# Attention results leave through device memory by head dimension and are normalised there, in an AdaLN block with attention and a mixture of experts

## What is computed

```python
h = layernorm(x) * (1 + ca) + sa
x = x + ga * attention(h)            # 2 x 2048 tokens, 16 heads of 16, causal
h = layernorm(x) * (1 + cb) + sb
x = x + gb * mixture(h)              # 8 experts, 512 tokens each

scores = relu(q @ k.T) * R_hat       # R_hat depends on the distance and the head
attn = softmax(where(causal, -inf, scores) / 4)
ctx = attn @ v ; ctx = ctx @ Wo + bo
```

## Time and profile before

| | us |
|---|---|
| median of 3 runs | 1761.94 (1759.61 to 1763.59) |
| the profiled execution's own time | 1759.48 |
| its span, first to last instruction | 1757.7 |
| busy in it: TensorE, VectorE, ScalarE, POOL | 1481.0, 1182.5, 1022.6, 931.5 |

### The profile page before, as it was taken

How to read it: one execution, slowest core, us unless ns; L and a number is a source line. 1 busy time by engine, 2 the same in 40 slices (tenths; PEclk the granted TensorE clock), 3 DMA queues, 4 the chain that set the end, 5 groups by cost and what they waited for, 6 DMA issues and landing times. The chain is left out here.

```text
span 1757.7 us, 43162 instructions
## 1 busy us (share of the span) xinstructions
PE 1481.0 (84%) x16098; PEld 1137.3 (65%) x16318; DVE 1182.5 (67%) x3764; ACT 1022.6 (58%) x1796; POOL 931.5 (53%) x1460
## 2 busy tenths in 40 slices
PE   5977999999999999999999998999985514999897
PEld 3544777777777777777777777777764304566565
DVE  7626778777877788778877787778749883122121
ACT  3435777777777777777777777777745500211211
POOL 3324766676567756676667666765656401223322
PEclk9987999999999999999999999999997655999999
DMA  6342121112211221121112211121022231334431
GB/s 206 112 143 97 60 80 58 50 54 82 61 50 52 78 64 53 50 78 64 55 50 67 72 58 50 55 81 62 2 97 81 96 120 26 75 78 106 113 81 21
DMA packets 68587, 129.06 MB, mean 73 GB/s; under 512 B 9392, under 2 KB 52288, under 8 KB 64288
## 3 DMA queue, kind: packets, MB, share of 16 engines
q1 hardware_dynamic: 60688, 115.38, 21.0%
q0 software_dynamic: 6464, 9.29, 3.0%
q10 hardware_dynamic: 1232, 1.71, 0.3%
HBM read 100.91 MB, written 25.44 MB: 72 GB/s over the span
## 5 line engine op out<-in xcount | busy, mean ns | idle before, releaser
L719 ACT ACTIVATE region_p<-turn_ps 128x512 f32<-128x512 f32 x512 | 303.6, 602 | 175.7 <-PE turn_ps L678 170.5
L719 ACT ACTIVATE region_o<-turn_ps 128x512 f32<-128x512 f32 x576 | 339.7, 601 | 110.5 <-PE turn_ps L678 105.1
L667 PE MATMUL score_ps<-region_s 128*128 128x384 bf16 (+3 forms) x1060 | 347.0, 347 | 33.1 <-DVE maxima L752 29.4
L678 PE MATMUL turn_ps<-ident,region_a 128*128 128x128 f32 x2048 | 342.4, 274 | 27.7 <-DVE region_c L772 22.7
L678 PE MATMUL turn_ps<-ident,region_x 128*128 128x128 f32 x2048 | 343.3, 275 | 26.3 <-DVE region_c L772 17.9
L794 POOL TENSOR_SCALAR region_a<-region_a,maxima 128x1152 f32<-128x1152 f32 (+6 forms) x224 | 271.9, 1214 | 125.7 <-ACT region_a L726 112.7
L752 DVE CUSTOM_DVE_ANT_0 region_x<-score_ps,region_t,maxima 128x512 f32<-128x512 f32 (+1 forms) x416 | 281.4, 707 | 74.5 <-PE score_ps L667 73.0
L678 PEld LDWEIGHTS turn_ps<-ident,region_a 128*128 128x128 f32 x2048 | 259.3, 141 | 58.8 <-DVE region_c L772 28.0
L678 PEld LDWEIGHTS turn_ps<-ident,region_x 128*128 128x128 f32 x2048 | 254.0, 141 | 60.4 <-DVE region_c L772 29.9
L752 DVE CUSTOM_DVE_ANT_0 region_a<-score_ps,region_t,maxima 128x512 f32<-128x512 f32 (+1 forms) x352 | 241.3, 699 | 47.0 <-remote 27.7
L752 DVE CUSTOM_DVE_ANT_0 region_a<-score_ps,region_t 128x384 f32<-128x384 f32 (+2 forms) x256 | 139.1, 553 | 87.9 <-PE score_ps L667 87.9
(11 more groups left out here) (198 smaller groups left out, 2104.1 us busy)
## 6 DMA issues: line engine op xcount, KB each, us to landing
region_t<-factor_rows SPq DMA_DIRECT2D x32, 1024.0 KB
region_x<-in_fc_t SPq DMA_DIRECT2D x16, 1024.0 KB, 8.1
region_s<-q_split SPq DMA_DIRECT2D x64, 192.0 KB
region_s<-k_split SPq DMA_DIRECT2D x64, 192.0 KB
region_x<-in_x SPq DMA_DIRECT2D x8, 1024.0 KB, 11.7
q_split<-region_o SPq DMA_DIRECT2D x16, 384.0 KB, 2.7
k_split<-region_t SPq DMA_DIRECT2D x16, 384.0 KB, 2.6
region_s<-q_split SPq DMA_DIRECT2D x32, 128.0 KB
```

Of the source, the lines that this page charges most:

```text
L667: nc.tensor.matmul(score_ps[:, j % SB, 0:(hi - lo) * P], stacks[:, b, 0, t * P:(t + 1) * P], stacks[:, b, 1, lo * P:hi * P], start=True, s ...
L678: last = nc.tensor.transpose(turn_ps[:, ring_at[what, j] % TB, q * P:(q + 1) * P], rows[t][:, k * P:(k + 1) * P], ident[:, :])
L719: nc.scalar.activation(weight(j), turn_ps[:, ring_at[what, j] % TB, :], ACT.Exp).then_inc(exp_done, 1)
```

## The change

The results of a group are no longer turned back. After `save`, SP stores the 17 rows of each stream to a tensor `heads_out` (head, 16 dimensions and sum, token) in device memory, 4 DMAs a group. They are read back as `context`, now laid out by model dimension (128 partitions) and token, with every sum repeated for its 16 partitions by a broadcasting read, and VectorE divides there: one reciprocal and one multiply of 128x1024 for each of eight groups of 512 tokens. The projection takes this layout as it is.

Events and places:

- `back`, `recip`, `norm` and `wait_ring` go. A turn waits only for the exponential three rounds earlier.
- `save` waits for the stores of two groups earlier.
- SP issues `dump` and `load` in the order of the same clock. At head 8 it reads the first eight heads back (8 DMAs); in head 15 after group 1 it reads the rest and the sums for batch element 0 (12 DMAs); after group 2 it loads three quarters of x.
- At the end of its attention list, VectorE normalises the four groups of element 0. Those of element 1 are read at the start of the mixture and normalised in its steps.
- The front has 4 + 8 steps instead of 5 + 8; TensorE's context transposes and ScalarE's copies of them go, and the projections have two pairs of PSUM buffers.

```diff
+        heads_out = dram("heads_out", (H, HD + 1, TOK), F32)
-        context = region_c[:, :].rearrange("p (t d) -> p t d", d=D)
+        context = region_c[:, :].rearrange("p (g k t) -> p g k t", g=NG, k=KC)
+        def load_sums(sp, g, k):
+            src = heads_out[k * (H // KC):(k + 1) * (H // KC), HD, g * GW:(g + 1) * GW]
+            src = bass.AP(tensor=src.tensor, offset=src.offset, ap=[src.ap[0], [0, HD], src.ap[1]])
+            sp.dma_start(sums_of[g][:, k * GW:(k + 1) * GW], src).then_inc(ld_heads[g], 16)
+        def normalise(nc, dve, g, inverted):
+            done = g % (NG // B) + 1
+            dve.wait_ge(ld_heads[g], HEADS_LOADS)
+            nc.vector.reciprocal(sums_of[g], sums_of[g]).then_inc(inverted, 1)
+            dve.wait_ge(inverted, done)
+            both = context[:, g, :, :].rearrange("p k t -> p (k t)")
+            nc.vector.tensor_tensor(both, both, sums_of[g], ALU.mult).then_inc(ctx_normed, 1)
...
-    events += [(back_time[g], "back", g) for g in range(GROUPS)]
-    events += [(back_time[g] + 0.6, "recip", g) for g in range(GROUPS)]
-    events += [(back_time[g] + 1.7, "norm", g) for g in range(GROUPS)]
+    events += [((g + 1) * ROUNDS - 1 + PV_LAG + 1.4, "dump", g) for g in range(GROUPS)]
+    events += [(due[last_of[b]] + 1, "load", b) for b in range(B)]
...
+                elif what == "dump":
+                    sp.wait_ge(pv_saved, h * GROUPS + (FREE_SAVED + j + 1))
+                    for q in range(STREAMS):
+                        long, short = (j // 2 * BT + t[j % 2][q] for t in (firsts, seconds))
+                        dst = heads_out[h, 0:HD + 1, long * P:(long + 1) * P]
+                        dst = bass.AP(tensor=dst.tensor, offset=dst.offset, ap=[dst.ap[0], [(short - long) * P, 2], dst.ap[1]])
+                        sp.dma_start(dst, sums[VW * q:VW * q + HD + 1, j % 2, :, :]).then_inc(dumped[j % 2], 16)
...
-                    wait_ring(pe, what, j, h)
+                    pe.wait_ge(exp_done, h * NR + (FREE_EXP + j + 1 - TB))
...
             over_heads(emit)
+            for g in range(NG // B):
+                normalise(nc, dve, g, inverted)
...
         @block.tensor
-            for s in range(G + 5):
+            for s in range(G + 4):
                 if s < G:
                     g = s
-                    for k in range(KC):
-                        if g:
-                            pe.wait_ge(ctxt_done, KC * (g - 1) + k + 1)
-                        for i in range(GT):
-                            last = nc.tensor.transpose(ctx_ps[k][:, i * P:(i + 1) * P],
-                                                       context[:, g * GT + i, k * P:(k + 1) * P], ident[:, :])
-                        last.then_inc(ctx_turned, 1)
+                    pe.wait_ge(ctx_normed, g + 1)
+                    if g >= 2:
+                        pe.wait_ge(x2_done, g - 1)
...
         @block.vector
-            for s in range(G + 5):
+            for s in range(G + 4):
+                if 0 <= s - 1 < G:
+                    rest_of_norm(0, s - 1, rstd1_done)
                 if 0 <= s - 2 < G:
-                    rest_of_norm(0, s - 2, rstd1_done)
-                if 0 <= s - 3 < G:
-                    rest_of_norm(1, s - 3, rstd2_done)
+                    rest_of_norm(1, s - 2, rstd2_done)
...
                     norm(1, g, h2)
+                if GB <= s + 1 < G:
+                    normalise(nc, dve, s + 1, inverted)
```

More of the change, by code:

```diff
@@ L486, in attention @@
     region_x, region_a, region_o, region_p = (o[k] for k in ("region_x", "region_a", "region_o", "region_p"))
-    vals, context, ident = o["vals"], o["context"], o["ident"]
+    x, vals, ident, heads_out = o["x"], o["vals"], o["ident"], o["heads_out"]
+    dumped, load_heads, load_sums, load_x2, normalise = (o[k] for k in ("dumped", "load_heads", "load_sums", "load_x2", "normalise"))
+    DUMPED = o["DUMPED"]
     stacks, factors, vblock, loaded, load_head = (o[k] for k in ("stacks", "factors", "vblock", "loaded", "load_head"))
@@ L621, in wait_top, with over_heads @@
             eng.wait_ge(scaled, h * NS + (FREE_SCALED + slots_of[n][-1] + 1))
[L623 to L638, removed]
+        def over_heads(emit):
+            for _, what, j, h in order_of_all:
+                emit(what, j, h)
         @block.sync
@@ L642, in _, with emit @@
             load_head(sp, 0, 1)
[L643 to L647, removed]
-        def over_heads(emit):
-            for _, what, j, h in order_of_all:
-                emit(what, j, h)
+            def emit(what, j, h):
+                if what == "load" and h < H - 1:
+                    sp.wait_ge(scaled, h * NS + (FREE_SCALED + last_of[j] + 1))
+                    load_head(sp, h + 1, j)
+                elif what == "dump":
[5 more added lines that the diff above has]
+                        sp.dma_start(dst, sums[VW * q:VW * q + HD + 1, j % 2, :, :]).then_inc(dumped[j % 2], 16)
+                    if (h, j) == (H // KC, 0):
+                        for i in range(2):
+                            sp.wait_ge(dumped[i], DUMPED * B * h)
+                        for g in range(NG):
+                            load_heads(sp, g, 0)
+                    if (h, j) == (H - 1, 1):
+                        sp.wait_ge(scaled, h * NS + (FREE_SCALED + last_of[0] + 1))
+                        for i in range(2):
+                            sp.wait_ge(dumped[i], DUMPED * (B * h + 1))
+                        for g in range(NG // B):
+                            load_heads(sp, g, 1)
+                            for k in range(KC):
+                                load_sums(sp, g, k)
+                    if (h, j) == (H - 1, 2):
+                        sp.wait_ge(turned, FREE_TURNED + H * NR - ROUNDS)
+                        for i in range(3):
+                            load_x2(sp, x, i)
+            over_heads(emit)
         @block.tensor
@@ L695, in emit @@
                     last.then_inc(pv_done, 1)
[L696 to L701, removed]
             over_heads(emit)
@@ L759, in emit @@
                     nc.vector.tensor_scalar(row, row, 0.0, top(j), ALU.max, ALU.subtract).then_inc(shifted, 1)
[L760 to L771, removed]
-                        last = nc.vector.tensor_tensor(context[:, at:at + STREAMS, bass.ds(h * HD, HD)], src,
-                                                       inv.unsqueeze(2).to_broadcast([P, STREAMS, HD]), ALU.mult)
-                    last.then_inc(norm_done, 1)
             over_heads(emit)
+            for g in range(NG // B):
+                normalise(nc, dve, g, inverted)
         @block.gpsimd
@@ L923, in _ @@
         def _(sp):
-            XQ = NT // 4
-            for i in range(4):
-                sp.dma_start(xs[:, i * XQ:(i + 1) * XQ, :],
-                             x[i * XQ * P:(i + 1) * XQ * P, :].rearrange("(t p) d -> p t d", p=P)).then_inc(ld_x[i], 16)
+            load_x2(sp, x, 3)
+            for i in range(2):
+                sp.wait_ge(dumped[i], DUMPED * B * H)
+            for g in range(GB, G):
+                load_heads(sp, g, 1)
+                for k in range(KC):
+                    load_sums(sp, g, k)
             for g in range(G):
```

133 lines of the change are left out of this document (64 added, 69 removed).

## The result

| | before | after |
|---|---|---|
| median in the same comparison, us | 1762.45 (1759.61 to 1763.59) | 1776.95 (1776.85 to 1777.5) |
| span of the profiled execution, us | 1757.7 | 1775.2 |

What follows compares the result with a forecast made beforehand. TensorE was taken to bound attention and VectorE the mixture's front. Terms -32 + 14.4 - 3 + 43 = +22.4 us on the profiled 1759.5 gave 1781.9; with the median 2.5 above, 1784 us, range 1764 to 1798.

Steps and rivals of the forecast that it cites:

- Attention: Removing TensorE's waits for VectorE's division: 31 after groups 1 and 3 at 1.03 us each, the others nothing; -32 us.
- the first kind: TensorE's waits for VectorE's division after query groups 0 and 2; ScalarE is late next, so removal was costed at nothing.
- The rival in which the first kind pays as well: In attention, waits after groups 0 and 2 also pay: 31 us more come back, 1753 us; chance 0.13.
- The gap: From VectorE's last score piece to the mixture: four normalisations of 7.8 us, 31.3 us against 17.1 us; +14.4 us.
- so they keep ahead: At attention's end, sums are read at 282 GB/s, 2.8 us per group, ahead of VectorE's normalisations.
- The start of the front: With x loaded early, first addition at 6.7 us, second between 10.8 and 13.2; -3 us (bounds -4 and -1.5).
- so I take the lower: First projection of the front: after 16 us idle TensorE runs at the lower clock, 6.5 us instead of 3.6.
- The four steps: Front, addition of group 3 to group 7: normalisations and waits for projections make steps 22.6 us; +43 us (+33 to +48).
- The rival with full clock: TensorE at full clock in the front: +33 in place of +43 us, 1774 us; chance 0.2.
- The stores: SP's 256 DMAs after the saves in attention, costed at nothing; bounds nothing and 16 us.
- if SP were late there is 30 us of cover: Copies out and read-back on SP cost nothing; a late SP would have 30 us of cover.

Runs made afterwards that it cites:

- e3: Kernel before, with the division of the turned-back block ordered earlier on VectorE after query groups 0 and 2 alone: 1760.55 us, ratio 0.9994.
- e4: Kernel before, with the division of the turned-back block ordered earlier on VectorE after query groups 1 and 3 alone: 1736.66 us, ratio 0.9864.
- e5: Changed kernel without the eight reciprocals of 128x1024, VectorE multiplying by the sums themselves: 1744.07 us, ratio 0.9897 to the kernel before.
- e8: Kernel before, with all divisions ordered earlier on VectorE and three quarters of x loaded at the end of attention: 1734.37 us, ratio 0.9847.
- e1: Changed kernel, with each normalisation of the front issued one step earlier on VectorE: 1754.16 us, ratio 0.9956 to the kernel before.
- e6: Kernel before plus the change's 256 stores, saves waiting for them and nothing reading them; turning back stays: 1766.26 us, ratio 1.0022.
- e7: e1 with each sum inverted once before it is repeated, stored and read back sixteenfold, VectorE then only multiplying: 1738.74 us, ratio 0.9868 to the kernel before.

## Why the prediction was right

**Attention, -32 predicted, -33.8 measured.** The choice was to price 31 waits at 1.03 us and 31 at nothing, because after the first kind the next releaser was ScalarE, late by itself. e3 and e4 bear out the two halves (1.3 and 23.9 us), and the row of e3 shows the wait in its new place. The rival in which the first kind pays as well is refuted. The sizes fit as well: the prediction's 1.03 us was 0.80 of waiting and 0.22 of transposes, and 31 x 0.80 = 24.8 us is what e4, which keeps the transposes, should give (23.9). With them the change should give 32 and gave 33.8, or 1.09 us each; the transposes were not taken away alone, so their share of 0.22 us each is argued and not shown.

**The gap, +14.4 predicted, +15.5 measured.** Reciprocals 6.55 us (predicted 6.56), multiplies 1.22 to 1.38. The one thing missed is the 1.20 us in which VectorE stood idle for the first sums: "so they keep ahead" was wrong for the first group by that much. Both of its premises were too kind. The prediction let the reads follow the save, 13.6 us before the last score piece; SP first waited for the stores to land and issued the first read at 1236.29, 7.2 us before it. And e5, where no reciprocal hides them, has the sums of the later groups 3.86 us apart and not 2.8 (0.79 MB each, 204 GB/s by this estimate, where 282 had been taken). The reciprocals' 6.5 us cover that. The rule cited from the Trainium skill, page "VectorE: DVE Perf Modes" (section "Walkthrough: the 8-slice pipeline in each mode"), disagrees: by the estimate from its eight repeats a reciprocal would take 8.5 us, and all eight took 6.5.

**The start of the front, -3 predicted, -4.6 measured.** The first addition came 5.4 us in, where 6.7 was predicted, and the second 10.1 us in, under the 10.8 to 13.2; the -4.6 lies outside the bounds of -4 and -1.5. That x came early is worth most of it, 3.7 us by e8's profile. The step that was mis-sized is "so I take the lower": TensorE had idled for 17.89 us, but the three projections that follow took 12.54 us together, at a granted clock of 0.81, and not 6.5 each:

```profile
1276.24 12.54 PE L995 MATMUL bank<-wo_gated,region_c 128*128 128x256 f32 x48 [17.89 <-PEq L628]
```

**The four steps, +43 predicted, +41.0 measured.** The steps were 21.28, 22.72, 21.60 and 22.74 us, 22.6 predicted. All of its parts stood, except two that were sized from one row each. The projections took 5.3 to 6.5 us, not 6.7. ScalarE's standardisation made VectorE wait for 0.17 us, not 1.2: the transposes of h2 had been priced at the lower clock (1.97 us) and ran in 1.04 us, since the projection in front of them had brought the clock up. The trace of before had said so: its transposes took 1.97 us only without a projection in front. e1 shows the mechanism: the order alone gave 22.8 us back. e5 shows the price of the work: 25.5 us for the four reciprocals in the steps. The rival with full clock is refuted by the projections' times.

**The rest.** 1.7 us at the start were not predicted and have no cause in the change: the start of attention lies between 144.8 and 149.7 us over all kernels run here, with the same projections before it. It is why the spans differ by 17.5 us and the sum of the four predicted terms is 18.1. The prediction's 22.4 us is thus 4.3 too high: 1.8 of it in attention, 1.6 at the start of the front, 2.0 in the steps, and 1.1 the other way in the gap. The median is 7.4 us under the sum's 1784.4: these 4.3, the 0.7 of the stretches that the prediction left out, and the 2.5 us by which it took the median to lie above the profiled execution, which the kernel after did not show (1777.04 us profiled, 1776.95 the median). So direction and mechanism came out, and every term within 2 us; the total of 22 us was half as large again as the 14.5 us between the medians.

**The stores.** Priced at nothing. For those inside attention e6 bears that out. For the last four, "if SP were late there is 30 us of cover" held for the change: SP was late, its last stores were issued until 21.8 us behind the last score piece, and four normalisations of 31 us covered that. e7 shows what lies under the cover as soon as VectorE is quicker: a gap 12 us longer than before. e5's gap, some 7 us longer than planned, has another cause in the main, the save that POOL delayed.

## What to carry to other kernels

A total of waits is not a price. Go from each kind of wait to the next instruction of that engine that somebody else releases: where that one is late too, the wait only moves (31 waits of 1 us, 1.3 us in all), and where it isn't, most of it is paid back (31 waits, 29.8 us, gave 23.9). Before a wait is removed by another data path, look whether the instruction that ends it can be ordered earlier: here one number gave 26 us, and the new path, which took away the same waits, cost 14.5.

In a pipeline of several engines, work that produces the input of another engine must not stand directly before the instruction that takes that engine's output; one step earlier the kernel was 22.8 us faster, with the same work. And invert before you repeat: VectorE's reciprocal costs 6.4 ns for each element of a partition, so a sum repeated for 16 partitions is paid 16 times. And take away an engine's work only after a look at what its next instructions run beside: without the reciprocals the multiplies fell on POOL's last masks and held them up.

## What the runs showed of the hardware

- A store is issued late when loads are queued in front of it. SP's queue in the kernel after, with four stores of one group each before the loads of x and behind them:

```profile
1231.40 1.52 SPq L669 DMA_DIRECT2D heads_out<-region_o  x4
...
1247.22 5.70 SPq L669 DMA_DIRECT2D heads_out<-region_o  x4
1252.97 4.88 SPq L128 DMA_DIRECT2D region_x<-in_x  x3
1258.82 6.49 SPq L669 DMA_DIRECT2D heads_out<-region_o  x4
```

  Four stores take 1.52 us to issue, and 5.7 to 6.5 us once the reads of 3 MB are queued; e7 shows 7.59 us, and e5, where they come 4.5 us behind the last load's issue, 2.96 us. Not the transfer alone waits, the issuing engine does. Whether the bytes or the number of DMAs in front decide was not taken apart. That is the place where e7 lost most of what was expected of it.
- TensorE's clock differed between two neighbouring groups of instructions: behind 14.6 to 20 us of idle time the projections of the four steps took 5.3 to 6.5 us (3.62 us at full clock), and the transposes right behind each took 1.04 us, where they had taken 1.97 us in a row of before.
- The reciprocal's time goes by elements alone: 6.54 us for 1024, 3.55 for 544, 1.75 for 256, with or without POOL beside it.
- VectorE and POOL hold each other up. A 128x4 operation of VectorE with two inputs takes 0.16 us alone and 2.2 us beside POOL's tensor operations; a POOL operation on 128x1024 takes 1.12 us, and 2.19 us when a VectorE multiply of 1.23 us starts 0.03 us before it (e5).
